# A 32-byte tile ahead of the weights in a cross-attention kernel on one core

## The chip, the core and the metric

The kernel runs on one core of a Trainium2 chip. The metric is the device time of one execution in microseconds. The core has a matrix engine (TensorE, PE in the profile; its weight loads are shown apart as PEld), a vector engine (DVE), a scalar engine (ACT), GpSimd (POOL) and a queue that only issues transfers (SP). Their common working memory, SBUF, has 128 partitions; a tile takes the same byte range in every partition.

## What is computed

The reference, cut to what matters. There are 64 batch elements, each with 256 text rows of 512 numbers and 256 context rows of 384 numbers, all in float32:

```python
text_p  = x   @ W_text  + b_text          # 512 -> 512
audio_p = ctx @ W_audio + b_audio         # 384 -> 512
Q = layer_norm(text_p, g1, beta1)
K = layer_norm(audio_p, g2, beta2)
alpha = softmax(Q @ K.T / sqrt(512))
out = layer_norm((alpha @ audio_p) @ W_out + b_out + x, g_out, beta_out)
```

## The kernel before

Two batch elements make one step, so there are 32 steps. Every product is made three times over at reduced width: each float32 operand is split into a high and a low part in the type fp32r (4 bytes an element), and the kernel adds high x high, high x low and low x high. So nearly every large tile comes in a pair, `xT_hi` and `xT_lo`, `wt_hi` and `wt_lo`, and so on. ACT makes the high parts, DVE the low ones, except for `xT_lo` of all steps but the first: there ACT writes the negated high part (L511) and GpSimd issues a transfer that adds `xT_in` to it (L1098).

One step of TensorE is: the projection of the context, K (`project_k`, 4 blocks of 9 matmuls, moving operand `cT_hi` or `cT_lo` of 512 columns, stationary operand a 128x128 block of `wa_hi` or `wa_lo`); the projection of the text, Q (`project_q`, 4 blocks of 12 matmuls, `xT_*` against `wt_*`, 512 columns); then for the step before, probabilities times context (`probs_context`, 36 matmuls of 256 columns, `pT_*` against `c_*`) and the output product (`output_part`, 36 matmuls of 512 columns, `wao_*` against `pcT_*`); and the scores (`scores`, 48 matmuls of 256 columns, `kT_*` against `qT_*`). Two further matmuls a step (`mean_squares`, L334) spread a sum of squares over all partitions with the stationary tile `mean_of`. The work of the steps is queued by hand on each engine and tied together by semaphores.

The moving operand of `probs_context` is not one run. Its columns are read through this view, which picks runs of 32 elements, 128 bytes each, with gaps between them:

```python
def turned(of, b, s):
    return of[:].rearrange("p a (b l s) c -> p b s l a c", b=NB, l=LT)[:, b, s]
```

In the last step the same product is made from another layout (`turned_last`), in which the 256 columns are one run of 1024 bytes. A few products are made in plain float32: the folding of `W_audio` into `W_out` (L397, moving operand `y_rows`), the folded bias (L405) and the transposes (L299, moving operand `ident`).

The tiles are placed in SBUF in the order of their declarations, each on the next multiple of 32 bytes. Ahead of the first weight tile, `wt_hi`, stand `ident` (512 bytes a partition), `neg_half` (16), `neg_one` (4), `mean_of` (512) and `eps` (4), and ahead of those things of the system that end on a multiple of 64. In the program as built `ident` begins at byte 16512 of each partition, `mean_of` at 17088, `wt_hi` at 17632 and `xT_in` at 65120. Between the weights and `xT_in` lie twelve small tiles of 8 to 16 bytes, which take 32 bytes each. All other large tiles are 2048, 4096, 6144 or 8192 bytes a partition.

Of the kernel before, what the change touches and what calls it, by code (L numbers as in the profile page):

```python
# [14 lines left out]
P = 128  # L15
# [3 lines left out]
def cross_attention_kernel(nc, x_rows, xT, c_rows, cT, w_text, b_text, w_audio, b_audio, w_out, b_out,  # L19
# [13 lines left out]
    with ExitStack() as stack:  # L33
        def sb(name, shape, dt=F32):
            return stack.enter_context(nc.sbuf_tensor(name, shape, dt))
# [9 lines left out]
        neg_half, neg_one = sb("neg_half", [P, T]), sb("neg_one", [P, 1])  # L45
        mean_of = sb("mean_of", [P, P], F32R)
        eps = sb("eps", [P, 1])

        wt_hi, wt_lo = sb("wt_hi", [P, DT, H], F32R), sb("wt_lo", [P, DT, H], F32R)
        wa_hi, wa_lo = sb("wa_hi", [P, CT, H], F32R), sb("wa_lo", [P, CT, H], F32R)  # L50
# [1178 lines left out]
```

How the kernel before makes its waits and increments, by code:

```python
        def wait(eng, semaphore, value):  # L157
            if not isinstance(value, int) or value > 0:
                eng.wait_ge(semaphore, value)
# [1 line left out]
        def wait_apart(eng, semaphore, value):  # L162
            if not isinstance(value, int) or value > 0:
                eng.wait_ge(semaphore, value)
                eng.sem_inc(passed, 1)
# [16 lines left out]
        @block.sync  # L184
# [48 lines left out]
            def step(i, odd, first=False, last=False):  # L233
                if first:
                    wait_apart(sp, cT_split, CT)
                    load_cT(1)
                    sp.wait_ge(x0_split, DT)
                elif not last:
                    wait_apart(sp, xT_split, 16 * i)
                if last:
                    sp.wait_ge(xT_split, 16 * (N - 1))
                    sp.dma_start(last_rows[:], x_rows[N - 1]).then_inc(x_last, 16)
                else:
                    load_xT(i + 1)
                if first:
                    sp.wait_ge(wao_done, CT)
                elif isinstance(i, int) and i == 1:
                    sp.wait_ge(bao_done, 1)
                if not isinstance(i, int) or i >= 2:
# [20 lines left out]
            run_steps(sp, step)  # L270
            for ready, count, t in ((rows_ready, 1, 2), (pool_ready, 1, 0), (rows_ready, 2, 3), (pool_ready, 2, 1)):
                sp.wait_ge(ready, count)
                sp.dma_start(out[N - 2, :, t, :], y_rows[0][:, t, :]).then_inc(stored[t], 16)
# [127 lines left out]
            def fold_bias():  # L401
                pe.wait_ge(q_centred, HT)
                for h in range(HT):
```

## Time and profile before

| | us |
|---|---|
| median of 3 runs (1273.39 to 1273.81) | 1273.65 |
| the profiled execution, its own time | 1272.33 |
| span of the profiled execution | 1270.5 |
| TensorE busy | 1251.0 |
| VectorE busy | 1078.2 |
| ScalarE busy | 1053.8 |
| GpSimd busy | 547.4 |

The span is what the profiler saw from the first to the last instruction; the execution's own time has another 1.8 us around it. Busy time of TensorE counts a pipelined matmul from its start to its end, so two matmuls in a row overlap; how fast TensorE works is read from the distance between the starts of successive matmuls.

### The profile page before, as it was taken

The numbers are of one execution on the slowest core, as the hardware profiler recorded it, in microseconds if no ns is written. First come the engines' busy times: TensorE is split into PE (matmuls) and PEld (weight loads), VectorE is DVE, ScalarE is ACT, GpSimd is POOL, SyncE is SP. The second block draws the span as 40 slices with busy tenths as digits, with TensorE's granted clock in tenths as the row PEclk, the third lists the DMA queues.
The fourth block names the chain that finished last, engine by engine and source line by source line (L and its number), as shares of the span: only waits on it lengthen the run. The fifth ranks groups of instructions, "written<-read, shape, count | busy, mean of one in ns | idle before, by whom it ended". The sixth has DMA issues, their size and how long they took to land.

```text
span 1270.5 us, 22559 instructions
## 1 busy us (share of the span) xinstructions
PE 1251.0 (98%) x6648; PEld 1067.6 (84%) x6648; DVE 1078.2 (85%) x1726; ACT 1053.8 (83%) x1789; POOL 547.4 (43%) x545
## 2 busy tenths in 40 slices
PE   6999999999999999999999999999999999999997
PEld 5688888888888888888888888888888888888886
DVE  6678888988888988888888888888889888889888
ACT  6787888888888988888888888888888888888884
POOL 0113554335544335544345544345544355543356
PEclk9999999999999999999999999999999999999999
DMA  7257766768767678776678667688677687677793
GB/s 257 60 163 226 224 189 187 188 204 239 225 172 200 185 217 239 211 180 196 184 228 239 202 170 198 194 235 235 180 190 186 204 244 222 179 192 188 210 236 104
DMA packets 99013, 253.53 MB, mean 200 GB/s; under 512 B 12336, under 2 KB 28208, under 8 KB 90800
## 3 DMA queue, kind: packets, MB, share of 16 engines
q1 hardware_dynamic: 77632, 187.22, 42.1%
q0 software_dynamic: 21360, 66.06, 28.9%
q8 instruction: 10, 0.16, 0.1%
q14 instruction: 11, 0.09, 0.0%
HBM read 137.38 MB, written 49.81 MB: 147 GB/s over the span
## 4 chain that ended last, share of the span: by engine, by line
PE 95%; DVE 2%; DMA 1%; ACT 1%; SPq 1%; issue 0%; DVEq 0%; ACTq 0%; POOLq 0%
PE wide L328 9%; PE wide L327 9%; PE wide L324 9%; PE score L292 7%; PE score L294 7%; PE score L293 7%; PE wide L382 7%; PE wide L381 7%; PE wide L380 7%; PE wide L294 7%; PE wide L292 7%; PE wide L293 7%; PE turn L293 1%; PE turn L294 1%; PE turn L292 1%; PE turn L334 1%
## 5 line engine op out<-in xcount | busy, mean ns | idle before, releaser
L1121 POOL TENSOR_TENSOR y_rows<-y_rows,betao_row 128x512 f32<-128x512 f32 x120 | 167.0, 1391 | 332.5 <-ACT y_rows L583 219.4
L324 PE MATMUL wide<-xT_hi,wt_hi 128*128 128x512 f32 x512 | 202.1, 395 | 2.5 <-ACT k_cols L543 1.3
L328 PE MATMUL wide<-xT_hi,wt_lo 128*128 128x512 f32 x512 | 202.2, 395 | 0.0
L327 PE MATMUL wide<-xT_lo,wt_hi 128*128 128x512 f32 x512 | 201.9, 394 | 0.0
L292 PE MATMUL wide<-cT_hi,wa_hi 128*128 128x512 f32 x384 | 152.4, 397 | 0.0
L542 ACT ACTIVATE squares<-wide,bac_col 128x512 f32<-128x512 f32 x128 | 88.2, 689 | 77.3 <-PE wide L294 77.3
L294 PE MATMUL wide<-cT_hi,wa_lo 128*128 128x512 f32 x384 | 152.1, 396 | 0.0
L293 PE MATMUL wide<-cT_lo,wa_hi 128*128 128x512 f32 x384 | 151.9, 396 | 0.0
L382 PE MATMUL wide<-wao_hi,pcT_lo 128*128 128x512 f32 x372 | 146.7, 394 | 0.0
L380 PE MATMUL wide<-wao_hi,pcT_hi 128*128 128x512 f32 x372 | 146.6, 394 | 0.0
L381 PE MATMUL wide<-wao_lo,pcT_hi 128*128 128x512 f32 x372 | 146.5, 394 | 0.0
L292 PE MATMUL score<-kT_hi,qT_hi 128*128 128x256 f32 x512 | 145.3, 284 | 1.0 <-DVE qT_lo L823 1.0
L294 PE MATMUL score<-kT_hi,qT_lo 128*128 128x256 f32 x512 | 144.7, 283 | 0.0
L293 PE MATMUL score<-kT_lo,qT_hi 128*128 128x256 f32 x512 | 144.7, 283 | 0.0
L1104 POOL TENSOR_TENSOR c_lo<-c_kept,c_hi 128x384 fp32r<-128x384 f32 x128 | 126.1, 1008 | 19.4 <-ACT c_hi L516 19.4
L1098 POOL DMA_DIRECT2D xT_lo<-xT_in x31 | 27.8, 897 | 233.3 <-ACT xT_lo L511 233.3
L324 PEld LDWEIGHTS wide<-xT_hi,wt_hi 128*128 128x128 f32 x512 | 96.5, 189 | 26.1 <-issue 2.0
L328 PEld LDWEIGHTS wide<-xT_hi,wt_lo 128*128 128x128 f32 x512 | 96.4, 188 | 22.4
L327 PEld LDWEIGHTS wide<-xT_lo,wt_hi 128*128 128x128 f32 x512 | 96.3, 188 | 21.2
L574 ACT ACTIVATE qT_hi<-q_cols,beta_col 128x512 fp32r<-128x512 f32 x128 | 90.7, 725 | 28.0 <-DVE q_cols L817 25.3
L823 DVE SCALAR_TENSOR_TENSOR qT_lo<-q_cols,beta_col,qT_hi 128x512 fp32r<-128x512 f32 x128 | 102.4, 800 | 8.5
L292 PEld LDWEIGHTS score<-kT_hi,qT_hi 128*128 128x128 f32 x512 | 97.9, 191 | 3.2 <-DVE qT_lo L823 1.6
(145 smaller groups left out, 3505.0 us busy)
## 6 DMA issues: line engine op xcount, KB each, us to landing
xT_in<-in_xT SPq DMA_DIRECT2D x32, 1024.0 KB, 8.9
xT_lo<-xT_in POOLq DMA_DIRECT2D x31, 1024.0 KB, 8.9
y_rows<-in_x_rows SPq DMA_DIRECT2D x124, 256.0 KB, 4.1
y_rows<-bao_row POOLq DMA_DIRECT2D x31, 1024.0 KB, 9.5
out<-y_rows SPq DMA_DIRECT2D x124, 256.0 KB, 3.3
cT_in<-in_cT SPq DMA_DIRECT2D x32, 768.0 KB, 8.7
c_kept<-in_c_rows SPq DMA_DIRECT2D x32, 768.0 KB, 7.4
p_out<-probs SPq DMA_DIRECT2D x31, 512.0 KB, 4.6
```

Of the source, the lines that this page charges most:

```text
L292: nc.tensor.matmul(to, a_hi, b_hi, start=(m == 0), stop=False)
L293: nc.tensor.matmul(to, a_hi, b_lo, start=False, stop=False)
L294: done = nc.tensor.matmul(to, a_lo, b_hi, start=False, stop=(m == n - 1))
L324: nc.tensor.matmul(wide[h][:], wt_hi[:, d, cols], xT_hi[:, d, :], start=(d == 0), stop=False)
L327: nc.tensor.matmul(wide[h][:], wt_hi[:, d, cols], xT_lo[:, d, :], start=False, stop=False)
L328: done = nc.tensor.matmul(wide[h][:], wt_lo[:, d, cols], xT_hi[:, d, :], start=False, stop=(d == DT - 1))
L380: nc.tensor.matmul(wide[t][:], hi, wao_hi[:, d, :], start=(d == 0), stop=False)
L381: nc.tensor.matmul(wide[t][:], hi, wao_lo[:, d, :], start=False, stop=False)
L382: done = nc.tensor.matmul(wide[t][:], lo, wao_hi[:, d, :], start=False, stop=(d == CT - 1))
L823: nc.vector.scalar_tensor_tensor(out=lo[:, h, :], in0=cols[:, h, :], scalar=shift[:, h:h + 1], in1=hi[:, h, :].bitcast(F32), op0=ALU.add, ...
L1104: nc.gpsimd.tensor_tensor(c_lo[:, t, :], c_kept[:, t, :], c_hi[:, t, :].bitcast(F32), ALU.subtract).then_inc(c_split, 1)
L1121: nc.gpsimd.tensor_tensor(rows, rows, betao_row[:], ALU.add).then_inc(y_ready, 1)
```

## The change

One tile of 8 float32 numbers a partition, 32 bytes, is declared after `eps` and ahead of `wt_hi`. No instruction reads or writes it. Every tile declared after it begins 32 bytes later.

```diff
         mean_of = sb("mean_of", [P, P], F32R)
         eps = sb("eps", [P, 1])
+
+        line_fill = sb("line_fill", [P, 8])
 
         wt_hi, wt_lo = sb("wt_hi", [P, DT, H], F32R), sb("wt_lo", [P, DT, H], F32R)
         wa_hi, wa_lo = sb("wa_hi", [P, CT, H], F32R), sb("wa_lo", [P, CT, H], F32R)
```

## Rows read from the trace of the kernel before

**Rows 1.** The page: busy time, and shares in 40 slices of the span.
```profile
PE 1251.0 (98%) x6648; PEld 1067.6 (84%) x6648; DVE 1078.2 (85%) x1726; ACT 1053.8 (83%) x1789; POOL 547.4 (43%) x545
...
PEclk9999999999999999999999999999999999999999
DMA  7257766768767678776678667688677687677793
```

**Rows 2.** The chain that ended last: shares of the span by engine.
```profile
PE 95%; DVE 2%; DMA 1%; ACT 1%; SPq 1%; issue 0%; DVEq 0%; ACTq 0%; POOLq 0%
```

**Rows 3.** All waits of TensorE: us in total, times, longest.
```profile
PE wide L299 <- DMA k_cols<-in_L_xattn_W_audio: 5.7, 1, 5.7
PE turn L334 <- DVE sq_parts L747: 1.9, 1, 1.9
PE wide L324 <- ACT k_cols L543: 1.3, 1, 1.3
PE wide L324 <- DMA xT_lo<-xT_in: 1.2, 1, 1.2
PE score L414 <- DMA beta_col<-in_L_xattn_beta: 1.2, 1, 1.2
PE score L292 <- DVE qT_lo L823: 1.0, 2, 0.7
```

**Rows 4.** Matmuls in order of time, start us and duration: Q, then probabilities times context.
```profile
603.05 0.39 PE L324 MATMUL wide<-xT_hi,wt_hi 128*128 128x512 f32 x1
...
614.44 0.28 PE L292 MATMUL score<-pT_hi,c_hi 128*128 128x256 f32 x1
...
618.76 0.39 PE L380 MATMUL wide<-wao_hi,pcT_hi 128*128 128x512 f32 x1
```

**Rows 5.** The same view: first score matmul and the matmul after the last.
```profile
627.35 0.28 PE L292 MATMUL score<-kT_hi,qT_hi 128*128 128x256 f32 x1
...
633.09 0.39 PE L292 MATMUL wide<-cT_hi,wa_hi 128*128 128x512 f32 x1
```

**Rows 6.** The same view: the last step's product, unbroken runs.
```profile
1250.61 0.28 PE L294 MATMUL turn<-pT_hi,c_lo 128*128 128x256 f32 x1
...
1254.69 0.39 PE L475 MATMUL wide<-wao_hi,pcT_hi 128*128 128x512 f32 x1
```

**Rows 7.** Groups of weight loads: count, busy us, mean ns; idle time before.
```profile
L292 PEld LDWEIGHTS score<-kT_hi,qT_hi 128*128 128x128 f32 x512 | 97.9, 191 | 3.2 <-DVE qT_lo L823 1.6 <-issue 0.2
L327 PEld LDWEIGHTS wide<-xT_lo,wt_hi 128*128 128x128 f32 x512 | 96.3, 188 | 21.2
L334 PEld LDWEIGHTS turn<-sq_parts,mean_of 128*128 128x128 f32 x64 | 12.0, 187 | 7.8 <-DVE sq_parts L747 2.9 <-issue 0.2
```

**Rows 8.** The chain in order of time: start us, length us, what.
```profile
35.95 6.88 PE wide L397 x16
...
53.77 11.36 DMA xT_lo<-xT_in
```

**Rows 9.** Groups of ScalarE and VectorE of like size, reading SBUF or PSUM.
```profile
L506 ACT CAST xT_hi<-xT_in 128x512 fp32r<-128x512 f32 x128 | 74.6, 608 | 3.9 <-DMA xT_in<-in_xT 3.9
L537 ACT CAST pcT_hi<-turn 128x512 fp32r<-128x512 f32 x31 | 18.2, 586 | 2.2
L565 ACT ACTIVATE turn<-turn 128x512 f32<-128x512 f32 x64 | 37.2, 582 | 2.0
L747 DVE TENSOR_TENSOR cT_lo<-cT_in,cT_hi 128x512 fp32r<-128x512 f32 x96 | 65.9, 686 | 25.6 <-ACT cT_hi L521 25.5
L747 DVE TENSOR_TENSOR pcT_lo<-score,pcT_hi 128x512 fp32r<-128x512 f32 x62 | 42.9, 692 | 3.7
```

**Rows 10.** The tile xT_lo from 590 to 680 us: its adding transfers.
```profile
L1098 POOL DMA_DIRECT2D xT_lo<-xT_in x3: 891/891/891, 592.3 to 669.1; - x3
...
DMA to landing us min/median/max: 8.9/8.9/8.9
```

## The prediction

> **What bounds the kernel.** I read the page first. TensorE is busy 98% of the span, at a granted clock of nine tenths or more in each slice, the upper of its two levels, 2.4 GHz [rows 1]. VectorE (85%) and ScalarE (83%) are some way behind. The reader should then see that the chain that ended last is TensorE for 95% [rows 2], and that TensorE's own waits come to 12.3 us in the whole span, all of them once or twice, at the beginning or the end of the program [rows 3]. So the kernel takes as long as its 6648 matmuls take to follow each other. A change pays if it changes the distance between the starts of matmuls, or the few microseconds at the two ends.
>
> That distance is read in order of time. From 603.05 to 614.44 us lie 48 matmuls of Q and one of `mean_squares`, all of 512 columns: 11.39 / 49 = 232.4 ns each [rows 4]. From 627.35 to 633.09 lie 48 score matmuls of 256 columns: 5.74 / 48 = 119.6 ns each [rows 5]. At 2.4 GHz and one column a cycle, 512 columns are 213.3 ns and 256 are 106.7 ns. So the fp32r matmuls stand 19.1 and 12.9 ns above one column a cycle. Whether this surplus has to do with where the operands begin is the whole question of this change.
>
> **The change part by part.** It adds no instruction, no wait and no transfer, and it takes none away. It moves addresses. `wt_hi` goes from 17632 = 275.5 x 64 to 17664 = 276 x 64. The six weight tiles and the three rows after them are multiples of 2048 bytes, the twelve small tiles take 12 x 32 = 384 = 6 x 64 bytes, so `xT_in` goes from 65120 = 1017.5 x 64 to 65152 = 1018 x 64, and all later large tiles go the same way. Before, every large operand begins in the middle of a 64-byte piece; afterwards each begins on the edge of one. `ident` and `mean_of` are on an edge already and don't move. Distances between the large tiles stay, so nothing that depends on two operands' relative places changes. Small column tiles swap places, half of them onto an edge and half off it.
>
> *Moving operands.* If TensorE fetched aligned pieces of 64 bytes, a 1024-byte run off the edge would need 17 pieces, a run on the edge 16. The trace of before has a test of this. `probs_context` reads its 256 columns as 8 runs of 128 bytes. Each run, off the edge, touches 3 pieces where 2 would hold it, 24 in all against the 17 of a single run. The 36 matmuls from 614.44 to 618.76 take 4.32 / 36 = 120.0 ns each [rows 4]. The scores, one run, take 119.6 ns [rows 5], and the same product in the last step, from one run, takes 34 matmuls from 1250.61 to 1254.69, 4.08 / 34 = 120.0 ns [rows 6]. So seven more pieces cost between 0 and 0.4 ns, one piece at most 0.06 ns. The change saves one piece an operand: 6592 fp32r matmuls x 0.06 = 0.4 us at the most. I take 0.
>
> *Stationary operands.* `mean_of` is on the edge, the others off it. Its weight load takes 187 ns, that of `wt_hi` 188, that of `qT_hi` 191 [rows 7]; and the stretch of Q that holds it has the usual distance. Even 1 to 4 ns here would lie under the matmul before it (232 or 120 ns apart). I take 0. With no cover at all it would be 6592 x 2.5 = 16 us, but loads of 188 ns already fit in distances of 120, so they are covered.
>
> *ScalarE and VectorE.* Tiles in PSUM stay where they are. ScalarE takes 608 ns from SBUF to SBUF, 586 from PSUM to SBUF and 582 within PSUM; VectorE 686 with both inputs in SBUF and 692 with one in PSUM [rows 9]. So at most 26 ns of a ScalarE instruction and nothing of VectorE's could be the price of lying off an edge. In the steady part this is hidden under TensorE. On the chain these two have 3% of 1270.5 = 38 us, some 54 instructions of 700 ns: a bound of 54 x 26 ns = 1.4 us for the gain. Nothing in the rows suggests a loss. I take 0.
>
> *Transfers.* Each row of a tile is now placed 32 bytes on. The transfer that has least room is the one that adds `xT_in` to `xT_lo`: issued at 592.3, landed 8.9 us later at 601.2 [rows 10], wanted by the first Q matmul at 603.05 [rows 4]. The room is 1.85 us, 21% of its length; a small change of its pace either way is hidden. I take 0.
>
> The sum is 1272.33 (the profiled execution) + 0, bounded by -1.8 and 0; the median of the runs is 1.3 us above that execution, so I predict their median, 1273.65, with 1271.5 to 1275.5 as this case's own range.
>
> **The rivals.** *First, the surplus is the price of the misplaced operand at full reading rate.* It could be that a 64-byte fetch starts wherever the run starts and straddles two pieces each time, at one array cycle a fetch. The comparison above doesn't exclude this: 8 runs of 128 bytes and one run of 1024 have the same 16 straddling fetches. It would explain 32 x 0.417 = 13.3 of the 19.1 ns, and 6.7 of the 12.9 ns. For it speaks also that the surplus is that of fp32r alone: the float32 matmuls of the folding, with a moving operand equally off the edge, take 6.88 / 16 = 430 ns for 512 columns at two cycles each (426.7), a surplus of 3 [rows 8]. They ask for their columns at half the rate, so a straddle could hide. Against it: from 256 to 512 columns the surplus grows by 6.2 ns only, where straddling fetches would have it double; half of it is the same whatever the length, as if each matmul paid it once. Its price: 3904 matmuls of 512 columns x 13.3 ns = 52 us, 2688 of 256 x 6.7 = 18 us, together 70, that is 1204 us. VectorE's 1078 and ScalarE's 1054 us would still fit below that.
>
> As a wider form, all of the surplus above that of float32 could go: 16.1 and 9.9 ns, 63 + 27 = 90 us, that is 1184 us. A page of the Trainium skill, "TensorE: Matmul & The Clock Gate", section on the back-to-back issue gap, gives the start-to-start distance of warm matmuls as N/2.4 plus about 2.5 ns; the float32 rows agree with it, and the fp32r rows stand 16.6 ns above it. By that rule alone this surplus is something that can be taken off, and the time would be near 1180.
>
> *Second, one piece an operand does count.* At the rate of the stream a piece of 64 bytes is 16 columns or 6.7 ns, and 6592 x 6.7 = 44 us would make 1230. By that price the broken runs would stand 47 ns above the whole ones, and they don't [rows 4 to 6]. Only a smaller price of the start alone, some nanoseconds, is left, since both layouts pay at least one start.
>
> *Third, on the other side: transfers get slower in their new places and `xT_lo` comes late.* The first of these transfers lasted 11.36 us and TensorE then did wait for it [rows 8], once for 1.2 us [rows 3]. If each of the 31 lasted that long, it would be 2.46 - 1.85 = 0.6 us late each, 19 us in all: 1293. It decides from 21% more than now. Against it: a transfer is 128 rows of 8192 bytes, and 32 bytes of shift touch no more than the ends of a row.
>
> The Trainium skill has a rule here that speaks against the change, in "DMA: Bandwidth & Descriptors", on how a descriptor splits into AXI transactions: the pieces begin on multiples of 256 bytes. By it, a row of 8192 bytes that begins 128 instead of 96 bytes past such a multiple (65152 against 65120) costs 260 beats instead of 259, and one of 2048 bytes 68 instead of 67, far below the 21% that would be needed. No row here shows the beats.
>
> *Fourth, the change doesn't do what it says*, because an unused tile is dropped. Its time is that of my forecast.
>
> **How the numbers follow.** No change, 0.62, with the fourth rival in it. The straddling fetch at 1204 us, 0.15, and its wider form near 1184, 0.05. A small or partial gain between 1210 and 1270, 0.09. The late transfer or another slowing, 0.09. I take 0.2% (2.5 us) as what a measurement of this kernel can tell from no change. Faster 0.29, same 0.62, slower 0.09. The likeliest is 1273.6 us. A range that leaves out no more than 2 in 10 has to reach to the straddling fetch, since no change and a partial gain alone hold 0.71: from 1201 to 1277.
>
> **What the profile after would show.** Right: Q at 232 ns a matmul, scores and `probs_context` at 120, the same six waits of TensorE. The straddling fetch: 219 and 113 ns, with the float32 matmuls still at 430, since the first stage's 512-column products would be the only ones not to move. A late transfer: a wait of the Q matmul L324 for the transfer into `xT_lo` some thirty times. I am wrong if the distance between matmuls moves at all; the weak point is that no fp32r moving operand of before begins on an edge, so the trace has no direct comparison.

## The result and the profile after

The changed kernel takes 1274.71 us, the median of 22 runs (1273.76 to 1276.67), beside 1272.47 us for 22 runs of the kernel before (1271.95 to 1275.06). The ratio over the runs is 1.0015, 95% interval 1.0008 to 1.0021 (the two medians alone give 1.0018): slower by 0.15%, clear of its own uncertainty and below the 0.2% that I had taken as the least that can be told. A second measurement in the course of the experiments gave 1.0013 (1.0004 to 1.0021).

The page of the profile after, its head and the shares of the chain:

```profile
span 1273.6 us, 22559 instructions
...
PE 1254.1 (98%) x6648; PEld 1068.6 (84%) x6648; DVE 1078.3 (85%) x1726; ACT 1054.8 (83%) x1789; POOL 548.3 (43%) x545
...
PE 95%; DVE 2%; DMA 1%; ACT 1%; SPq 1%; issue 0%; DVEq 0%; ACTq 0%; POOLq 0%
```

TensorE's waits are those of [rows 3], 12.1 us now and 12.3 us before, but for 0.5 us at the beginning for `wa_lo`, which the list of before doesn't have. Three of them:

```profile
PE wide L301 <- DMA k_cols<-in_L_xattn_W_audio: 5.7, 1, 5.7
PE turn L336 <- DVE sq_parts L749: 1.9, 1, 1.9
...
PE wide L326 <- DMA xT_lo<-xT_in: 1.2, 1, 1.2
```

So no wait has come into the steps, and no transfer is late. The spans of the two profiles differ by 3.1 us, more than the runs do, and the part that isn't the change's can be read from stretches. Each line gives the stretch, its length, the busy time of each engine, the granted clock, the share of the transfers and their GB/s. Before, and below it after:

```profile
10.00:45.00 35.00, 31.82 (x111) 21.62 (x111) 25.45 (x43) 24.70 (x43) 1.29 (x1) 1.00 0.49 185
```
```profile
10.00:45.00 35.00, 31.97 (x108) 21.70 (x108) 24.13 (x42) 23.70 (x42) 1.29 (x1) 0.90 0.49 184
```

In this one execution the clock stood at its lower level for a while in the first 45 us, and its second step begins 1.4 us later than before (56.96 us against 55.52); the runs of either kernel fall into two groups that far apart. From 45 to 1236 us the granted clock is 1.00 in both, and the other 1.7 us of the 3.1 us are spread over the steps. Compared at the same step, in the rows that answer to [rows 4] and [rows 5] (start of a matmul, duration), after:

```profile
605.14 0.39 PE L326 MATMUL wide<-xT_hi,wt_hi 128*128 128x512 f32 x1
...
609.55 0.40 PE L336 MATMUL turn<-sq_parts,mean_of 128*128 128x512 f32 x1
...
616.55 0.28 PE L294 MATMUL score<-pT_hi,c_hi 128*128 128x256 f32 x1
...
620.87 0.39 PE L382 MATMUL wide<-wao_hi,pcT_hi 128*128 128x512 f32 x1
...
622.27 0.40 PE L336 MATMUL turn<-sq_parts,mean_of 128*128 128x512 f32 x1
...
629.48 0.28 PE L294 MATMUL score<-kT_hi,qT_hi 128*128 128x256 f32 x1
...
635.24 0.39 PE L294 MATMUL wide<-cT_hi,wa_hi 128*128 128x512 f32 x1
```

The two `mean_squares` matmuls of that step before the change:

```profile
607.47 0.39 PE L334 MATMUL turn<-sq_parts,mean_of 128*128 128x512 f32 x1
...
620.14 0.40 PE L334 MATMUL turn<-sq_parts,mean_of 128*128 128x512 f32 x1
```

Q takes 616.55 - 605.14 = 11.41 us against 11.39. Up to the first `mean_squares` matmul it is 4.41 against 4.42; so the loss is behind that matmul. The output product up to the second one takes 1.40 us against 1.38, the scores 5.76 against 5.74. Taken over the 28 middle steps, in nanoseconds from the start times of the trace (medians):

```
                                             before   after   difference
K, 36 matmuls                                  8364    8364        0
Q, 19 matmuls                                  4414    4412       -2
first mean_squares                              232     237       +5
Q, 29 matmuls                                  6739    6763      +24
probs_context, 36 matmuls                      4323    4325       +2
output product, 6 matmuls                      1382    1400      +18
second mean_squares                             234     233       -1
output product, 30 matmuls                     6970    6976       +6
scores, 48 matmuls                             5741    5757      +16
```

The differences add up to 68 ns. Not every step is at its median: the mean step is longer by 58 ns, and 31 x 58 = 1.8 us, near the 2.2 us between the medians of the runs. The place where the loss begins gave the decisive experiment, but only at the end.

Two of the parts have no fixed length. From the second step on the 29 Q matmuls take one of a few values between 6733 and 6764 ns, in either kernel: before, 6739 or 6740 ns in 25 steps, after, 6762 to 6764 ns in 24. `probs_context` goes with them; in two steps before the change it took 4360 ns. The 30 output matmuls and the scores are steadier: apart from the first step and the last, the scores never took more than 5746 ns before the change and never less than 5755 ns after it, the output matmuls never more than 6970 and never less than 6975.

### The profile page after: what moved, and what is told of

Its sections match the earlier page's. It is cut to its first block, busy times and chain, and to the rows that moved or that the text cites. A ratio compares the mean times of both kernels' runs of the same rounds, so it can differ in the third digit from the quotient of the medians.

```text
span 1273.6 us, 22559 instructions
## 1 busy us (share of the span) xinstructions
PE 1254.1 (98%) x6648; PEld 1068.6 (84%) x6648; DVE 1078.3 (85%) x1726; ACT 1054.8 (83%) x1789; POOL 548.3 (43%) x545
## 4 chain that ended last, share of the span: by engine, by line
PE 95%; DVE 2%; DMA 1%; ACT 1%; SPq 1%; issue 0%; DVEq 0%; ACTq 0%; POOLq 0%
PE wide L330 9%; PE wide L329 9%; PE wide L326 9%; PE score L294 7%; PE score L295 7%; PE score L296 7%; PE wide L384 7%; PE wide L383 7%; PE wide L382 7%; PE wide L296 7%; PE wide L294 7%; PE wide L295 7%; PE turn L294 1%; PE turn L295 1%; PE turn L296 1%; PE turn L336 1%
```

## The experiments

Theory A is that the place of an operand within a 64-byte piece sets the time; theory B that any other program differs by as much; theory R that the distance between the two operands of a matmul sets it. Distance here means the address of the moving operand less that of the stationary one. Before the change it is 128 modulo 256 bytes for K, Q and the output product, and 0 for scores and `probs_context`. Theory M came last and is told with its two runs.

**Fills of other sizes.** Three kernels with an unused tile: one declared last, where it moves nothing, one of 64 and one of 96 bytes in the place of the change's 32.

```diff
+        line_fill = sb("line_fill", [P, 8])     # last32: behind row_inv
+        line_fill = sb("line_fill", [P, 16])    # fill64: ahead of wt_hi
+        line_fill = sb("line_fill", [P, 24])    # fill96: ahead of wt_hi
```

> The unused 32-byte tile is declared last, so no other tile moves. Theory A (the loss comes from where operands begin, on or off a multiple of 64 bytes): 1.000 of before, steady step 38.45 us. Theory B (any other program is placed and fetched differently, whatever its addresses): about 1.001 to 1.002. Theory C (places count, but not by 64): 1.000.

> The tile ahead of the weights is 64 bytes, so that all large tiles move but keep their old place within a 64-byte piece (wt_hi at 17696 = 276.5 x 64). Theory A: 1.000 of before, steady step 38.45 us. Theory B: 1.001 to 1.002. Theory C (any move of the tiles changes which places of SBUF are in use together): something other than 1.000, by some tenths of a per cent, either way.

> The tile ahead of the weights is 96 bytes; the large tiles begin on multiples of 64 as after the change, 64 bytes further on. Theory A: 1.0015 as after the change, steady step 38.51 us. Theory B: the same. Theory C: a value of its own, not bound to 1.0015.

Measured 0.9995 (0.9986 to 1.0004), 1.0004 (0.9995 to 1.0013) and 0.9995 (0.9986 to 1.0004). The fill of 96 bytes puts every large tile on a multiple of 64 like the change, and costs nothing that runs within 0.1% can tell. Theory A has fallen, B too; what the change costs belongs to its 32 bytes.

**The tile behind the weights, and the change again.**

```diff
         g2_col, beta2_col = sb("g2_col", [P, HT]), sb("beta2_col", [P, HT])
+        line_fill = sb("line_fill", [P, 8])     # behind_weights; 16 in behind64, 24 in behind96
         xT_in, cT_in = sb("xT_in", [P, DT, T * P]), sb("cT_in", [P, CT, T * P])
```

> The 32-byte tile is declared just ahead of xT_in: weights, the three rows and the small column tiles stay where they were, xT_in and all after it begin on multiples of 64. Theory A: if the moving operands and scores carry the loss, 1.0015; if the weight tiles or the small column tiles carry it, 1.000; with both, between. The matmuls of K (232.4 ns apart before and after) and the output product (231.8 to 232.3 before, 232.3 to 232.9 after) show which.

> The changed kernel once more, with nothing else changed, beside the others. If the loss of 0.15% belongs to the program: 1.001 to 1.002 again. If it belongs to the circumstances of the first measurement: 1.000.

> A tile of 64 bytes just ahead of xT_in: weights stay, all later tiles move by 64 bytes, so that the distance between the weight tiles and the moving tiles changes by 64. Theory R (the distance between the two operands of a matmul sets what they cost each other, with a period of 64 bytes): 1.000, K and Q matmuls 232.3 ns apart. If the period is longer: neither 1.000 nor the 1.005 of the 32-byte distance, K and Q matmuls at another value. Theory A (place within a 64-byte piece alone): 1.000.

> The same with 96 bytes, distance changed by 96. Theory R with a period of 64: 1.005, K and Q matmuls 234 ns apart as with 32 bytes. With a longer period: another value.

> 32 bytes ahead of the weights and 32 more ahead of xT_in: weights on multiples of 64, all later large tiles off them, distance changed by 32 as when the tile stood behind the weights alone. Theory R: 1.005, K and Q matmuls 234 ns apart. Theory A with the moving tiles to blame (they lie as before the change): 1.000. Theory A with the weights to blame: 1.001 to 1.002.

Measured 1.0048 (1.0035 to 1.0062) for `behind_weights`, 1.0013 for the change again, 1.0000 (0.9991 to 1.0009) for 64, 1.0028 (1.0017 to 1.0038) for 96, and 1.0052 (1.0039 to 1.0065) for 32 bytes ahead and 32 behind. In `behind_weights` the stretch from the first Q matmul to `probs_context` grows from 11.39 us to 11.47:

```profile
608.80 0.40 PE L326 MATMUL wide<-xT_hi,wt_hi 128*128 128x512 f32 x1
...
620.27 0.28 PE L294 MATMUL score<-pT_hi,c_hi 128*128 128x256 f32 x1
```

A shift between the weights and the moving tiles costs more than three times what the common shift of the change does, and `ahead_and_behind`, whose moving tiles lie off the edge, costs the same as `behind_weights`, where they lie on it. That is theory R. The period isn't 64, though: with 64 bytes K and Q stood about 1 ns wider than before, and the total came out even only because the output product, with the `mean_squares` matmul in it, became closer, 8.50 us instead of 8.59 (from 618.76 to 627.35 us in [rows 4] and [rows 5]):

```profile
620.50 0.39 PE L382 MATMUL wide<-wao_hi,pcT_hi 128*128 128x512 f32 x1
...
629.00 0.28 PE L294 MATMUL score<-kT_hi,qT_hi 128*128 128x256 f32 x1
```

In the output product the roles are the other way round: the weights `wao_*` are the moving operand and `pcT_*` the stationary one. A tile behind the weights therefore takes its bytes off this distance: 32, 64 and 96 bytes make 96, 64 and 32 of 128, where K and Q go to 160, 192 and 224.

**Distances by themselves.** A kernel in which only TensorE works, from two tiles that begin alike; it leaves out the attention. One line for each setting:

```diff
+            for n in range(96): made = nc.tensor.matmul(banks[1][:, 0:512], of(weights, 0, 128), of(moving, 128, 512), start=(n == 0), stop=(n == 95))
```

> Not the attention: one stream of fp32r matmuls, each with its own weight load, from two tiles that both begin at the same place of a 2048-byte stretch; nothing else runs, and the output is only a copy of x. One line for each setting of 96 matmuls: the weights at byte 0 and the moving operand at 0 to 480 in steps of 32; then both shifted together by 32 to 224 at a distance of 384; then both shifted by 0 to 96 at a distance of 0; then 256 columns. Theory A (place within a 64-byte piece): the lines with the moving operand or weights off a multiple of 64 differ from the others, in the shifted series too. Theory R (distance between the two operands): the first series varies by some ns, at 384 the shifted series is flat at about 232 ns a matmul, and 32 bytes more or less cost 1 to 2 ns. If neither matters without the other engines: all lines of 512 columns alike.

In order of time, start and length of each line's 96 matmuls; the start of the next line less its own, over 96, is the distance between matmuls:

```profile
44.71 21.92 PE L72 MATMUL bank<-moving,weights 128*128 128x512 f32 x96
66.47 22.57 PE L73 MATMUL bank<-moving,weights 128*128 128x512 f32 x96
88.88 22.15 PE L74 MATMUL bank<-moving,weights 128*128 128x512 f32 x96
110.86 22.57 PE L75 MATMUL bank<-moving,weights 128*128 128x512 f32 x96
133.27 22.56 PE L76 MATMUL bank<-moving,weights 128*128 128x512 f32 x96
155.67 22.64 PE L77 MATMUL bank<-moving,weights 128*128 128x512 f32 x96
178.15 22.55 PE L78 MATMUL bank<-moving,weights 128*128 128x512 f32 x96
200.54 22.55 PE L79 MATMUL bank<-moving,weights 128*128 128x512 f32 x96
222.93 21.93 PE L80 MATMUL bank<-moving,weights 128*128 128x512 f32 x96
244.70 22.57 PE L81 MATMUL bank<-moving,weights 128*128 128x512 f32 x96
267.10 22.15 PE L82 MATMUL bank<-moving,weights 128*128 128x512 f32 x96
...
557.49 21.96 PE L95 MATMUL bank<-moving,weights 128*128 128x512 f32 x96
579.29 21.96 PE L96 MATMUL bank<-moving,weights 128*128 128x512 f32 x96
601.08 21.96 PE L97 MATMUL bank<-moving,weights 128*128 128x512 f32 x96
...
644.67 11.67 PE L99 MATMUL bank<-moving,weights 128*128 128x256 f32 x96
656.18 11.48 PE L100 MATMUL bank<-moving,weights 128*128 128x256 f32 x96
667.49 11.47 PE L101 MATMUL bank<-moving,weights 128*128 128x256 f32 x96
678.80 11.55 PE L102 MATMUL bank<-moving,weights 128*128 128x256 f32 x96
690.19 11.67 PE L103 MATMUL bank<-moving,weights 128*128 128x256 f32 x96
```

| line | distance, bytes | ns from matmul to matmul |
|---|---|---|
| L72, L80 | 0, 256 | 226.7, 226.8 |
| L73, L81 | 32, 288 | 233.4, 233.3 |
| L74 | 64 | 229.0 |
| L75, L76 | 96, 128 | 233.4, 233.3 |
| L77 | 160 | 234.2 |
| L78, L79 | 192, 224 | 233.2, 233.2 |
| L95, L96 | 0, both operands at 0 and at 32 | 227.1, 227.0 |
| L99 to L102 | 0, 32, 64, 128, with 256 columns | 119.9, 117.8, 117.8, 118.6 |

The period is 256 bytes. L95 and L96 move both operands from an edge of a 64-byte piece to the middle of one and show nothing. The table also gives the full kernels' numbers to about half a nanosecond: `behind_weights` (160) had K and Q at 234.1 ns, `behind64` (192) at 233.4; the output product, at 96, 64 and 32 in `behind_weights`, `behind64` and `behind96`, stood at 233.1, 229.5 and 233.1. Only at 128, the distance of the kernel before, the full kernel's 232.3 ns is a nanosecond less than the table's 233.3; in the shifted series at that distance, lines of 232.3, 233.3 and 232.4 ns came in turn, again and again. So one distance can have more than one pace.

A page of the Trainium skill, "SBUF — State Buffer", section "Who interferes with whom", lists two independent read ports for TensorE, one for the moving operand and one for weight loads, and says that TensorE waits for nobody. The section is about engines that get into each other's way; of the two reads of TensorE it says that they are independent. With nothing else at work, the same two reads here cost between 226.7 and 234.2 ns a matmul by their distance alone; the measurement decides.

**The distance taken to 0.** The small column tiles are declared ahead of the weights, all of them, eight, or six of the twelve; no byte is added, and all large tiles stay off multiples of 64.

```diff
+        ba_col, bt_col = sb("ba_col", [P, HT]), sb("bt_col", [P, HT])
...
+        g2_col, beta2_col = sb("g2_col", [P, HT]), sb("beta2_col", [P, HT])
         wt_hi, wt_lo = sb("wt_hi", [P, DT, H], F32R), sb("wt_lo", [P, DT, H], F32R)
```

> The twelve small tiles are declared ahead of the weights instead of behind the rows: the weights move by 384 bytes, everything from xT_in on stays, all large tiles are off multiples of 64 as before, and the distance between weights and moving tiles goes from 384 to 0 modulo 2048. Theory A: 1.000. Theory R: another time, K, Q and the output product at another distance between matmuls, scores and probs_context unchanged at 120 ns.

> Eight of the twelve small tiles ahead of the weights, distance 128 modulo 2048, all large tiles off multiples of 64. Theory A: 1.000. Theory R: if the period is 128 or 256 bytes, 1.000 with K and Q at 232.3 ns; else another value.

> Six of the twelve small tiles ahead of the weights, distance 192 modulo 2048, all large tiles off multiples of 64. Theory A: 1.000. Theory R: a value of its own; if the period is 64 bytes, 1.000.

Measured 0.9883 (0.9866 to 0.9899), 0.9999 (0.9990 to 1.0008) and 0.9991 (0.9982 to 1.0001). In `small_ahead`:

```profile
PE 1237.2 (98%) x6648; PEld 1065.7 (85%) x6648; DVE 1083.2 (86%) x1726; ACT 1052.2 (84%) x1789; POOL 549.5 (44%) x545
```
```profile
597.43 0.39 PE L324 MATMUL wide<-xT_hi,wt_hi 128*128 128x512 f32 x1
...
608.62 0.28 PE L292 MATMUL score<-pT_hi,c_hi 128*128 128x256 f32 x1
...
612.98 0.39 PE L380 MATMUL wide<-wao_hi,pcT_hi 128*128 128x512 f32 x1
```

Q takes 11.19 us instead of 11.39, with its 512-column matmuls 227.3 ns apart. Moving eight tiles keeps 128 modulo 256 and changes nothing, moving all twelve gives 0 and 1.2%: it is the distance and not the order of the tiles. Moving six gives 192 for K and Q and 64 for the output product, the distances of `behind64`, and comes out about even as that did. `probs_context` is 0.04 us longer (4.36), which I had not expected and can't explain; it is a length that the kernel before has in two of its steps, and `last32` in half of them.

**Even placement at distance 0, and the 256-column products.**

```diff
+        line_fill = sb("line_fill", [P, 8])     # small_ahead_even: small_ahead, this ahead of ba_col
```
```diff
-        qT_hi, qT_lo = ...                      # spread32, spread64: small_ahead, and these three
-        probs = ...                             # lines declared behind pcT_hi, pcT_lo
-        pT_hi, pT_lo = ...
+        line_fill = sb("line_fill", [P, 16])    # 8 in spread32
+        qT_hi, qT_lo = ...
+        probs = ...
+        pT_hi, pT_lo = ...
```

> small_ahead with a 32-byte tile ahead of the weights: the two operands of the K, Q and output matmuls at a distance of 0 modulo 256, and now every large tile on a multiple of 64. Theory R: as small_ahead, 0.988 to 0.989, 227.3 ns. Theory A: some tenths of a per cent off that.

> small_ahead, and qT, probs and pT declared last behind a 32-byte tile, so that the distance of the two operands of the scores and of probs_context goes from 0 to 32 modulo 256, the others stay at 0. From the table of distances 256-column matmuls are 2.0 ns closer at 32 than at 0: 84 x 31 x 2.0 ns = 5 us below small_ahead, 0.984. If the broken runs of probs_context answer otherwise, only the scores gain: 3 us, 0.986.

> The same with 64 bytes. From the table the same 2.0 ns: 0.984; without probs_context 0.986.

Measured 0.9877 (0.9860 to 0.9893), 0.9885 (0.9868 to 0.9901) and 0.9854 (0.9838 to 0.9871), the last at a median of 1253.61 us beside 1272.85. The change's idea, applied where the distance is 0, again does nothing that these runs can tell. `spread64` is faster than either kernel; its scores take 623.68 - 618.02 = 5.66 us instead of 5.74:

```profile
618.02 0.28 PE L293 MATMUL score<-kT_hi,qT_hi 128*128 128x256 f32 x1
...
623.68 0.40 PE L293 MATMUL wide<-cT_hi,wa_hi 128*128 128x512 f32 x1
```

`spread32` missed both ratios that were expected of it, 0.984 and 0.986; `spread64` came between them. In `spread32` the scores came closer too (118.3 ns), but `probs_context` went up to 122 ns; its moving operand is read in broken runs, and the table was made with unbroken ones. The expectation also had the distance of the scores wrong: `qT`, which moved, is their stationary operand, so they went from 0 to 224 and, in `spread64`, to 192, while `probs_context` went to 32 and 64. The table has no line of 256 columns at 224 or 192.

**Where the loss of a common shift comes from.** First TensorE alone, at the kernel's own addresses and in its own order; the attention is left out.

```diff
+            for n, (m, w) in enumerate(Q * 3): made = nc.tensor.matmul(banks[1][:, 0:512], at(w + 32, 128), at(m + 32, 512), start=(n == 0), stop=(n == 3 * len(Q) - 1))
```

> Not the attention: only TensorE works, on tiles at exactly the addresses of the kernel before and with the operand order of its K, Q, output and score products (three times 36, 48, 36 and 48 matmuls, one line each), at a common shift of 0, 32, 64 and 96 bytes; the output is only a copy of x. If the 0.15% is TensorE's own (where both operands lie together), Q and output stand 0.2 to 0.6 ns wider at 32 than at 0, 64 and 96, K the same. If it comes from the other engines or transfers beside TensorE, all four shifts are alike.

The 144 Q matmuls at a shift of 0, and the line after them; then the same at 32:

```profile
76.09 33.76 PE L98 MATMUL bank<-high,low 128*128 128x512 f32 x144
109.69 25.36 PE L99 MATMUL bank<-low,high 128*128 128x512 f32 x108
...
177.35 33.76 PE L102 MATMUL bank<-high,low 128*128 128x512 f32 x144
210.95 25.36 PE L103 MATMUL bank<-low,high 128*128 128x512 f32 x108
```

33.60 us both times, 233.3 ns a matmul, and the same at 64 and 96. The common shift of the large tiles costs TensorE nothing in this stream, whose pace is the table's 233.3 ns and not the 232.3 ns of the full kernel. What this kernel doesn't have is `probs_context`, whose two operands move together, and `mean_squares`. Its stationary operand `mean_of` is declared ahead of the new tile and doesn't move, its moving operand `sq_parts` does: theirs is the only distance among the fp32r products that the change alters, from 160 to 192 modulo 256. Theory M blames it. The fills of 64 and 96 bytes had altered this distance as well, to 224 and 0, and cost nothing; so theory M has to say that 192 costs where 160, 224 and 0 don't. Two kernels tell it apart, one that changes this distance and moves no large tile (besides `mean_of` only `neg_one` moves, which TensorE doesn't read), one that moves all large tiles and keeps it.

```diff
-        neg_half, neg_one = sb("neg_half", [P, T]), sb("neg_one", [P, 1])
+        neg_half = sb("neg_half", [P, T])       # mean_of_alone
         mean_of = sb("mean_of", [P, P], F32R)
+        neg_one = sb("neg_one", [P, 1])
```
```diff
+        line_fill = sb("line_fill", [P, 8])     # all_moved
         ident = sb("ident", [P, P])
```

> neg_one is declared behind mean_of instead of ahead of it. mean_of begins 32 bytes earlier, no large tile moves, all of them stay off multiples of 64, and the distance from mean_of to sq_parts grows by 32 as in the changed kernel. Theory M (the loss of the change comes from the one pair of operands whose distance it altered, mean_of against sq_parts in the two mean_squares matmuls of a step, and from the pace that the matmuls behind it fall into): 1.001 to 1.002, Q up to the first mean_squares matmul as before, the 29 Q matmuls behind it 20 ns or so longer. If the places of the large tiles carry the loss: 1.000.

> The 32-byte tile is declared ahead of ident, so that mean_of moves with the large tiles: these lie on multiples of 64 exactly as after the change, but no distance between operands of the fp32r matmuls is altered. Theory M: 1.000. If the places of the large tiles carry the loss: 1.0015.

Measured 1.0014 (1.0005 to 1.0023) for `mean_of_alone` and 1.0001 (0.9992 to 1.0010) for `all_moved`. The intervals meet at their ends, but the runs lie apart: none of the eleven of `mean_of_alone` was under 1273.81 us, and five of the eleven of `all_moved` were under 1272.50. Theory M stands. `all_moved` has every large tile where the change puts it, and its step is that of the kernel before to the nanosecond in each of the nine parts of the table above:

```profile
604.97 0.39 PE L325 MATMUL wide<-xT_hi,wt_hi 128*128 128x512 f32 x1
...
616.36 0.28 PE L293 MATMUL score<-pT_hi,c_hi 128*128 128x256 f32 x1
...
629.27 0.28 PE L293 MATMUL score<-kT_hi,qT_hi 128*128 128x256 f32 x1
...
635.01 0.39 PE L293 MATMUL wide<-cT_hi,wa_hi 128*128 128x512 f32 x1
```

11.39 and 5.74 us again. In `mean_of_alone` the scores take 634.86 - 629.10 = 5.76 us as after the change:

```profile
629.10 0.28 PE L293 MATMUL score<-kT_hi,qT_hi 128*128 128x256 f32 x1
...
634.86 0.39 PE L293 MATMUL wide<-cT_hi,wa_hi 128*128 128x512 f32 x1
```

The 30 output matmuls are also those of after (6976 ns), and both hold in every step but the first and the last. But the 29 Q matmuls took 6744 ns, not 6763 or so as expected. Its profiled step is only 10 to 15 ns longer than before, which doesn't account for the 0.14% of its runs.

`small_ahead_even` has the distance 192 for `mean_squares` as well, beside 0 for K, Q and the output product, and its profiled step is not longer than that of `small_ahead`, where it is 160. So the pair doesn't seem to bring the loss in every surrounding; the ratios, 0.9877 and 0.9883 with intervals of 0.16% either way, can't tell.

## Why the prediction was wrong

The forecast was no change at 1273.6 us; the kernel came out at 1274.71, slower by 0.15%. That the two times are so near is in part luck: the median of three runs that the forecast stood on was 1.2 us above that of all 22 (1272.47), which is half of the loss. The range, 1201 to 1277, reached far down for the sake of a gain; that it holds 1274.71 says little for the working.

*Right.* The added tile is placed as described, and the ratios of the fill of 96 bytes, of all tiles moved, and of even placement at distance 0 show that beginning on a multiple of 64 costs and gives nothing, to about 0.1%: the 0 that I took for moving and stationary operands as such holds. The first rival (fetches that straddle two pieces, 1204 us), its wider form, and the second (a piece more or less, 1230) have fallen with theory A. The third had a part of the chance on the slower side, but its mechanism isn't there: the transfer into `xT_lo` keeps TensorE waiting once, as before. ScalarE's and VectorE's instructions and the float32 matmuls didn't change.

*The step that failed* is in the description of the moved addresses: "`ident` and `mean_of` are on an edge already and don't move. Distances between the large tiles stay, so nothing that depends on two operands' relative places changes." The first sentence holds the exception to the second. `mean_of` is an operand of two matmuls a step, and its partner moved. I had named the relative place of two operands as a thing that could matter, and then left out the one pair for which it changed. I also looked for the effect only in that matmul, in the "usual distance" of the stretch that holds it; it shows behind it, in 83 or so matmuls that have nothing to do with `mean_of`. The size is small: some 60 ns in a step of 38.4 us. The runs showed in place of the step that this one distance, gone from 160 to 192, is enough by itself for 1.0014.

*The profile had more than I took from it.* I set the surplus of 19 ns over one column a cycle against the place of each operand alone and found no row for it. The distance between the two operands was in the code, 128 modulo 256 everywhere in K, Q and the output product, and 5 of those 19 ns hang on it. Two readings were looser than they look. The price of a 64-byte piece, at most 0.06 ns, came from a single step; in other steps `probs_context` takes 4.36 us, 121.1 ns a matmul, which would allow 0.2 ns a piece and 1.4 us in all. And L397 has 24 records for its 12 products, so a float32 product of 512 columns is two records of 430 ns each.

*What stays open.* Why the distance matters at all is not shown; that both operands' reads meet in the same part of SBUF is a guess. Nor is it shown how one `mean_squares` matmul sets the pace of those behind it. The pace isn't fixed by addresses alone: `last32`, which moves nothing, went to and fro from step to step between 6740 and 6764 ns for the 29 Q matmuls and between 4305 and 4360 ns for `probs_context`, while its runs took as long as those of the kernel before beside it. And `mean_of_alone` was profiled in a milder pace than its runs imply: that execution took 1274.30 us, the median of its runs, but 1.7 us of it had passed before its second step began (57.23 us against 55.52). Matmul by matmul only a part of the loss belongs to the pair: 6 ns of the output matmuls and 16 ns of the scores, which are there in the three profiles with the distance 192 and all others as before (the changed kernel twice, and `mean_of_alone`) and in none of `before`, `last32` and `all_moved`. That is 22 of some 60 ns; for the rest the two ratios speak alone.

## What to carry to other kernels

Where TensorE is the bound with fp32r operands, look at the address of the moving operand less that of the stationary one, modulo 256 bytes, for each product: small tiles declared between two large ones decide it, and putting them elsewhere costs no bytes and no instructions and was worth 1.2% here, 1.5% together with distances of 192 for the scores and 64 for `probs_context`. Mind which operand is the moving one: in the output product it is the weights. Whether a tile begins on a multiple of 64 was worth nothing. When a tile is added, list which pairs of operands change their distance, with the small ones that stay behind, before calling the addition free.

## What the runs showed of the hardware

Back-to-back fp32r matmuls of 512 columns, each with its weight load, stand 226.7 to 234.2 ns apart by the distance of their operands, with a period of 256 bytes: best at 0, 229.0 at 64, 233 to 234 elsewhere. Shifting both operands together by 32, 64 or 96 bytes had no effect: 227.0 ns at distance 0, and 233.3 at distance 128 in the stream at the kernel's addresses. With 256 columns the order is another one: 119.9 ns at 0, 117.8 at 32 and 64, 118.6 at 128. And at one distance, 128, the stream was seen at 232.3, 232.4 and 233.3 ns; that this hangs on what ran before is a guess, but the addresses alone don't fix it, since one and the same kernel changes its pace from step to step.

Even at distance 0, 226.7 ns stay 11 above what the Trainium skill, "TensorE: Matmul & The Clock Gate", section on the back-to-back issue gap, gives for the gap of warm matmuls of 512 columns (about 216). The same section calls that the gap of single matmuls and gives 131 ns for a stream in which each has its weight load; no stream here comes near that, the closest is 226.7.
